# The second layer of a two-layer model run in halves of two blocks, with layer norm and routing of one half beside expert tiles of another

## The chip, the cores and the metric

One core of a Trainium2 chip runs the whole program in one launch. The metric is the device time in microseconds (us) from launch to end; the median of several runs is compared, and smaller is better. Everything is in float32, with each matrix product made of three matmuls on a high part and a low part of its operands (below).

## What is computed

The input is 2,048 tokens of width 128 (4 sequences of 512). Each of two layers adds half a feed-forward, a mixer, and half a feed-forward again to the residual `x`, each on a layer norm of `x`. In layer 0 the feed-forward is a dense one and the mixer a selective scan; in layer 1, which the change is about, they are 64 routed experts with shared ones, and causal attention with 8 heads:

```python
x = x + 0.5 * _L1_ffn_ref(_layernorm(x), ...)   # experts
x = x + _L1_attn_ref(_layernorm(x), ...)        # attention, each sequence of 512 by itself
x = x + 0.5 * _L1_ffn_ref(_layernorm(x), ...)   # the same experts again

rw = _route(x, gate_w, gate_bias)      # per token: best 4 of 8 groups, best 8 experts in them
expert_out = vmap(lambda gw, uw, dw: (silu(x @ gw.T) * (x @ uw.T)) @ dw.T)(Wg, Wu, Wd)
out = einsum('eth,te->th', expert_out, rw) + _mlp(x, Sg, Su, Sd)
```

All experts are computed for all tokens and weighted by `rw`, which is zero for those not chosen. 64 experts of 88 rows are taken as 44 chunks of 128 rows.

## The kernel before

The residual `x` stays in SBUF, 128 features by 2,048 tokens, cut into NB = 4 blocks of T = 512 tokens, one for each sequence. The program is six stages one after the other, with a barrier between them (`end_phase`, `start_phase`: each engine waits for the other four's last work): feed-forward, scan, feed-forward, experts, attention, experts. There is no scheduler: each engine's instructions stand in the order in which the code writes them, and semaphores tie them together.

**Split operands.** `split_hi` (ScalarE) copies a tile into its high part, `split_lo` (GpSimd, in places VectorE) writes full minus high, and `mm3` issues three matmuls (lines 219 to 221).

**The experts' tiles.** A tile is one chunk of 128 expert rows by one block of 512 tokens; an expert stage has 8 tiles of the shared experts and then 44 x 4 = 176 tiles. For tile t TensorE (PE) makes `gate` in PSUM bank 4, once `silu` of tile t-1 has read it, and `up` in bank 5, once `gated` of tile t-1 has read it, each three matmuls; then `down` of tile t-3 (AHEAD = 3), three more. ScalarE (ACT) makes `silu` (line 985); VectorE (DVE) makes `gated` = silu x up (line 1160) and `weighted` = gated x the token's weights in `rwb` (line 1171); ACT splits the high part, GpSimd (POOL) the low part, `e_lo` (line 227). The chunk's weights arrive in `e_raw` by DMA, and ACT and POOL split them into `eh` and `el`. The loop over chunk pairs has 8 tiles: two chunks (two buffers), each against four blocks.

**The start of an expert stage.** Nothing of it is made before the stage. TensorE does the layer norm (a matmul for the mean, small ones for the variance, a matmul to spread the deviation), of all four blocks or, in the first expert stage, of the last one, and the routing logits; then DVE makes the routing of all 16 groups of 128 tokens in 25 steps (lines 1102 to 1151), each of which waits for the one before it, with the 8 shared tiles between. TensorE turns the result, ACT writes it into `rwt`, SyncE (SP) stores it to memory and loads it back, one row spread over the expert's partitions, into `rwb`. The first expert tile waits for that.

**Attention** does the layer norm of all four blocks, then block by block 8 heads; `o_lo` is the low part of one head's output on POOL.

**Tables.** Silu, Sqrt, Sigmoid, Gelu and Exp are in tables of ACT; `load_table` brings one in by a tiny activation.

## Time and profile before

| | |
|---|---|
| time, median of 3 runs | 1790.04 us (1789.91 to 1793.42) |
| the profiled execution, its own time | 1788.16 us |
| its span, first to last instruction | 1786.4 us |
| TensorE matmul busy | 1614.6 us, 90% |
| VectorE busy | 1227.8 us, 69% |
| ScalarE busy | 955.5 us, 53% |
| GpSimd busy | 897.1 us, 50% |
| TensorE's granted clock, mean | 0.947 of 2.4 GHz |
| moved by DMA | 118.7 MB |

A busy share is a mean over stages that are limited by different things, so it is read stage by stage. A matmul of 512 columns shows as 0.39 us but the next one starts 0.23 us after it, so starts, and not durations, tell what one costs on TensorE. What an engine's idle time is worth is told by who waits for it.

### The profile page before, as it was taken

What the parts mean: (1) busy time and instruction counts of PE and PEld (TensorE: products, weight loads), DVE (VectorE), ACT (ScalarE), POOL (GpSimd) and SP (SyncE); (2) the same over time, 40 slices, a digit from 0 to 9 for tenths busy, and PEclk for the clock granted to TensorE, in tenths of its full rate; (3) what the DMA queues carried; (4) which work ended last, traced back from release to release, by engine and by line L of the source; (5) the groups of instructions that cost most, each with busy time, mean ns of one, the idle gap of its engine ahead of it and who ended that gap; (6) DMA issues with size and microseconds to landing.
All of it is one profiled execution on the core that took longest, in us unless ns stands there. A gap on an engine that the chain in (4) does not pass through costs nothing.

```text
span 1786.4 us, 25495 instructions
## 1 busy us (share of the span) xinstructions
PE 1614.6 (90%) x6840; PEld 1208.8 (68%) x6840; DVE 1227.8 (69%) x2015; ACT 955.5 (53%) x1866; POOL 897.1 (50%) x786
## 2 busy tenths in 40 slices
PE   8997577787899975999999998999998699999998
PEld 6775323333377754888888876898875488888887
DVE  5555699999755564666666666787766466666666
ACT  4344645454334342565656555777763256556565
POOL 1001076666410042777777773434323277777776
PEclk9998789999899987999999998999997699999999
DMA  2000000000000003666667640000000367767765
GB/s 102 10 0 1 0 1 1 0 0 0 7 1 1 0 36 84 147 150 152 146 154 150 144 105 1 1 0 0 0 10 1 91 144 152 152 147 152 148 150 120
DMA packets 30035, 118.72 MB, mean 66 GB/s; under 512 B 5323, under 2 KB 17059, under 8 KB 18211
## 3 DMA queue, kind: packets, MB, share of 16 engines
q1 hardware_dynamic: 29987, 118.15, 29.8%
q8 instruction: 22, 0.36, 0.1%
q14 instruction: 26, 0.21, 0.0%
HBM read 116.03 MB, written 2.10 MB: 66 GB/s over the span
## 4 chain that ended last, share of the span: by engine, by line
PE 66%; DVE 3%; issue 2%; POOL 2%; ACT 2%; DMA 1%; POOLq 0%; DVEq 0%; SPq 0%; ACTq 0%
PE ps L219 19%; PE ps L220 18%; PE ps L221 18%; PE ps L1292 2%; PE ps L1277 1%; PE ps L1279 1%; PE ps L1278 1%; PE ps L643 1%; POOL m_hc L853 1%; PE ps L242 1%; DMA rwb<-rw_rows 1%; PE ps L255 1%; POOL e_lo L227 1%; PE ps L249 1%; PE ps L1280 1%
## 5 line engine op out<-in xcount | busy, mean ns | idle before, releaser
L227 POOL TENSOR_TENSOR e_lo<-e_h,e_hi 128x512 fp32r<-128x512 f32 (+1 forms) x368 | 478.5, 1300 | 259.3 <-ACT e_hi L224 252.2
L1160 DVE TENSOR_TENSOR ps<-e_s,ps 128x512 f32<-128x512 f32 x352 | 245.1, 696 | 239.4 <-PE ps L221 179.8
L985 ACT ACTIVATE e_s<-ps 128x512 f32<-128x512 f32 (+1 forms) x368 | 220.5, 599 | 324.6 <-PE ps L221 324.5
L219 PE MATMUL ps<-xn_hi,eh 128*128 128x512 f32 x704 | 280.6, 399 | 22.6 <-DVE ps L1160 22.6
L220 PE MATMUL ps<-xn_lo,eh 128*128 128x512 f32 x704 | 280.8, 399 | 0.0
L221 PE MATMUL ps<-xn_hi,el 128*128 128x512 f32 x704 | 276.4, 393 | 0.0
L1171 DVE TENSOR_TENSOR e_h<-ps,rwb 128x512 f32<-128x512 f32 x352 | 243.3, 691 | 44.7 <-DMA rwb<-rw_rows 21.0
L224 ACT ACTIVATE e_hi<-e_h 128x512 fp32r<-128x512 f32 (+1 forms) x368 | 229.0, 622 | 47.5 <-DVE e_h L1171 25.5
L853 POOL TENSOR_TENSOR m_hc<-m_h,m_c 128x512 f32<-128x512 f32 x128 | 172.8, 1350 | 124.9 <-DVE m_h L809 122.5
L643 PE MATMUL ps<-m_hc,const 128*128 128x512 f32 x256 | 149.6, 667 | 48.8 <-POOL m_hc L853 43.9
L219 PEld LDWEIGHTS ps<-xn_hi,eh 128*128 128x128 f32 x704 | 133.7, 190 | 55.0 <-DVE ps L1160 24.8
L227 POOL TENSOR_TENSOR xn_lo<-ln_c,xn_hi 128x512 fp32r<-128x512 f32 (+1 forms) x24 | 32.9, 1370 | 273.8 <-ACT xn_hi L224 273.8
L221 PEld LDWEIGHTS ps<-xn_hi,el 128*128 128x128 f32 x704 | 134.1, 190 | 31.3
L220 PEld LDWEIGHTS ps<-xn_lo,eh 128*128 128x128 f32 x704 | 133.8, 190 | 31.5
L809 DVE TENSOR_TENSOR_SCAN m_h<-ln_t,ps 128x512 f32<-128x512 f32 x128 | 154.5, 1208 | 0.5 <-ACT ln_t L717 0.5
L219 PE MATMUL ps<-e_hi,eh 128*128 128x512 f32 x352 | 140.0, 398 | 2.4 <-POOL e_lo L227 2.4
L221 PE MATMUL ps<-e_hi,el 128*128 128x512 f32 x352 | 140.6, 399 | 0.0
L220 PE MATMUL ps<-e_lo,eh 128*128 128x512 f32 x352 | 136.8, 389 | 0.0
L219 PE MATMUL ps<-hid_hi,wh 128*128 128x512 f32 x288 | 122.1, 424 | 5.9 <-DVE hid_lo L227 5.0
L643 PEld LDWEIGHTS ps<-m_hc,const 128*128 128x128 f32 x256 | 40.2, 195 | 115.1 <-POOL m_hc L853 114.4
L221 PE MATMUL ps<-hid_hi,wl 128*128 128x512 f32 x288 | 113.1, 393 | 0.0
L220 PE MATMUL ps<-hid_lo,wh 128*128 128x512 f32 x288 | 113.0, 392 | 0.0
(239 smaller groups left out, 3180.5 us busy)
## 6 DMA issues: line engine op xcount, KB each, us to landing
rwb<-rw_rows SPq DMA_DIRECT2D x32, 704.0 KB
rwb<-rw_rows SPq DMA_DIRECT2D x40, 512.0 KB
e_raw<-in_experts SPq DMA_DIRECT2D x88, 192.0 KB, 5.5
rwb<-rw_rows SPq DMA_DIRECT2D x16, 640.0 KB
rwb<-rw_rows SPq DMA_DIRECT2D x24, 384.0 KB
rwb<-rw_rows SPq DMA_DIRECT2D x16, 448.0 KB
rwb<-rw_rows SPq DMA_DIRECT2D x16, 320.0 KB
rwb<-rw_rows SPq DMA_DIRECT2D x40, 128.0 KB
```

Source lines behind the costliest of these rows:

```text
L219: pe.matmul(out, w_hi, x_hi, start=start, stop=False, skip_group_check=True)
L220: pe.matmul(out, w_hi, x_lo, start=False, stop=False, skip_group_check=True)
L221: return pe.matmul(out, w_lo, x_hi, start=False, stop=stop, skip_group_check=True)
L224: return act.activation(hi, full, ACT.Identity)
L227: return eng.tensor_tensor(lo, full, hi.bitcast(F32), ALU.subtract)
L643: pe.matmul(ps[:, 4 + m, :], ident, m_hc[:, q % DEEP, :], start=(n == 0), stop=(n == DS - 1), skip_group_check=True).then_inc(M["y_sum"], 1)
L809: dve.tensor_tensor_scan(m_h[:, q % DEEP, :], m_da[:, q % DEEP, :], ps[:, B_BANKS[q % DEEP], :], 0.0, ALU.mult, ALU.add).then_inc(M["h"], 1)
L853: pool.tensor_tensor(m_hc[:, q % DEEP, :], m_h[:, q % DEEP, :], m_c[:, n % 2, :], ALU.mult).then_inc(M["hc"], 1)
L985: act.activation(e_s[0:rows_, buf, :], ps[0:rows_, 4, :], ACT.Silu).then_inc(S["silu"], 1)
L1160: dve.tensor_tensor(ps[0:rows_, 6 + buf % 2, :], e_s[0:rows_, buf, :], ps[0:rows_, 5, :], ALU.mult).then_inc(S["gated"], 1)
L1171: dve.tensor_tensor(e_h[:, j % 4, :], ps[:, 6 + j % 2, :], rwb[:, j // NB, cut(j % NB)], ALU.mult).then_inc(S["weighted"], 1)
L1292: last = pe.transpose(pt_at(kb)[:, (r - kb) * P:(r - kb + 1) * P], p32[:, r, kb * P:(kb + 1) * P], ident)
```

## The change

Layer 1 is run in halves of two blocks. The stages after the second feed-forward are now E1A (first experts, blocks 0 and 1), attention 0, E1B (first experts, blocks 2 and 3), attention 1, E2A (second experts, blocks 0 and 1), E2B (second experts, blocks 2 and 3). Layer norm and routing are made beside the tiles of the stage before:

- The second feed-forward also makes the routing of blocks 0 and 1 (on DVE after the splits of its blocks 2 and 3) and the logits of blocks 0 to 2; E1A makes the layer norm of block 3 and the routing of blocks 2 and 3; E1B both for blocks 0 and 1 of the second experts; E2A both for blocks 2 and 3.
- `beside(t)` on each engine puts a piece after tile t: means, variances and spreads in the free banks 2 and 3, logits after t = 14 and 15, routing on DVE in five pieces (`route_pairs`, `route_groups`, `route_mask`, `route_top`, `route_weights`) after t = 17, 18, 20, 21, 23 for one block and 26, 27, 29, 31, 32 for the other. A block's routing is 24 steps on 4 groups of tokens; before it was 25 steps on 16. The first SIDE = 4 rounds of 8 tiles are written out for it, and the others are a loop.
- A chunk now has two tiles and not four, and is loaded, and split, four times and not twice. There are four buffers. The low part of the down weights is now made by DVE (`down_low`), and that of gate and up stays with POOL. `rwb` holds 1,024 tokens a chunk.
- The attention's weights are split in 8 parts beside tiles of E1A, the low parts by DVE (`attention_low`).
- The layer norm of the first block of an attention half stands at the end of the experts before it, and that of its second block beside the attention's start. Attention and both feed-forwards are written out block by block instead of in loops.

```diff
-        TILES = 2 * NB + CH * NB
-        ROUTE_STEPS = 25
+        TILES = 4 + 2 * CH
+        ROUTE_STEPS = 24
...
+        SHARED, PER, AHEAD, SLOTS = 4, 8, 3, 4
+        ROUNDS = CH // SLOTS
+        SIDE = 4
...
             def beside(t):
+                if t == 7:
+                    if first in L[1]:
+                        one_deviation(act, L[0], first, 2)
+                    one_deviation(act, L[0], second, 3)
+                    load_table(act, ACT.Silu)
...
+                if t == 16:
+                    if first in L[1]:
+                        route_scores(act, R, first, 2)
+                    route_scores(act, R, second, 3)
+                    load_table(act, ACT.Silu)
...
+            def down_low(i, c):
+                dve.wait_ge(*S("wd_hi", SLOTS * i + c + 1))
+                split_lo(dve, el[:, c, 0, :], e_raw[:, c, 0, :], eh[:, c, 0, :]).then_inc(S["wd_lo"], 1)
...
+                if t in (17, 26):
+                    route_pairs(dve, R, first if t == 17 else second)
+                if t in (18, 27):
+                    route_groups(dve, R, first if t == 18 else second)
+                if t in (20, 29):
+                    route_mask(dve, R, first if t == 20 else second)
...
+            def round_(i):
+                for j in range(PER):
+                    tile(i, j)
+                    if j in (0, 2, 4):
+                        down_low(i, 1 + j // 2)
+                    if j == 6:
+                        down_low(i + 1, 0)
+                    if isinstance(i, int):
+                        beside(in_round(i, j))
...
-            moe_pe(pe, E1, LN[3], True)
+            moe_pe(pe, E1A, 0, R1, (LN[3], (3,)), (2, 3), LN4A)
             end_phase(pe)
             start_phase(pe, 4)
-            att_pe(pe, LN[4])
+            att_pe(pe, LN4A, 0)
             end_phase(pe)
             start_phase(pe, 5)
-            moe_pe(pe, E2, LN[5], False)
+            moe_pe(pe, E1B, 1, R2, (LN5A, (0, 1)), (0, 1), LN4B)
+            end_phase(pe)
+            start_phase(pe, 6)
+            att_pe(pe, LN4B, 1)
+            end_phase(pe)
+            start_phase(pe, 7)
+            moe_pe(pe, E2A, 0, R2, (LN5B, (2, 3)), (2, 3), None)
+            end_phase(pe)
+            start_phase(pe, 8)
+            moe_pe(pe, E2B, 1, R2, None, None, None)
             end_phase(pe)
```

VectorE before, in the first expert stage: steps of the routing of all blocks (`r_t`, `r_u`, `r_small`), with products of shared tiles (`e_h<-e_s,ps`) between, ahead of any expert tile.

```order
L1110 TENSOR_TENSOR r_u<-r_t 128x256 [waits moe_route]
L1076 TENSOR_TENSOR e_h<-e_s,ps 88x512 [waits moe_silu,moe_up]
L1111 TENSOR_TENSOR r_t<-r_t 128x256 [waits moe_route]
L1112 TENSOR_TENSOR r_t<-r_u 128x256 [waits moe_route]
L1113 TENSOR_TENSOR r_u<-r_u,r_t 128x256 [waits moe_route]
L1076 TENSOR_TENSOR e_h<-e_s,ps 88x512 [waits moe_silu,moe_up]
```

VectorE now, in E1B after tile 17: the first routing piece of block 0 stands between the products of expert tiles 17 and 18 (`ps<-e_s,ps` is `gated`, `e_h<-ps,rwb` is `weighted`), and a split of weights (`el<-e_raw,eh`, `down_low`) and the second piece behind tile 18.

```order
L463 TENSOR_TENSOR r_c<-r_s,rows 128x256 [waits route_scores]
L467 TENSOR_TENSOR r_t<-r_c 128x128 [waits route_route]
L468 TENSOR_TENSOR r_u<-r_c 128x128 [waits route_route]
L471 TENSOR_TENSOR r_u<-r_t 128x64 [waits route_route]
L472 TENSOR_TENSOR r_t<-r_t 128x64 [waits route_route]
L473 TENSOR_TENSOR r_t<-r_u 128x64 [waits route_route]
L1277 TENSOR_TENSOR ps<-e_s,ps 128x512 [waits moe_silu,moe_weighted,moe_up,route_route]
L1282 TENSOR_TENSOR e_h<-ps,rwb 128x512 [waits moe_rw_in3,moe_h_lo,moe_gated]
L234 TENSOR_TENSOR el<-e_raw,eh 128x128 [waits moe_wd_hi]
L477 TENSOR_TENSOR r_u<-r_u,r_t 128x64
```

What moved: steps a quarter as wide, but as many for each block, now stand in VectorE's queue ahead of the next tile's `gated`.

ScalarE now, in E1B after tile 16: two table loads (to Sigmoid and back to Silu) stand around the scores, between `e_hi` of tile 16 and `silu` (`e_s<-ps`) of tile 18.

```order
L231 ACTIVATE e_hi<-e_h 128x512 [waits moe_down,moe_weighted]
L1123 ACTIVATE eh<-e_raw 128x128 [waits moe_down]
L426 ACT_TABLE_LOAD
L426 ACTIVATE r_s<-ps 128x256 [waits route_logits] x2
L240 ACT_TABLE_LOAD
L240 ACTIVATE unused<-cols 128x1
L1129 ACTIVATE e_s<-ps 128x512 [waits moe_gated,moe_gate]
```

What moved: the scores of a stage (`r_s`) were made before its first tile, and their table was loaded where no `silu` waited.

TensorE now, at the end of E1A: the mean of block 0 for the attention ahead of the last `down`, its variance and spread behind it, and then the barrier.

```order
L361 MATMUL ps<-x,mean_w 128x512 [waits route_rwt,moe_x_new]
L226 MATMUL ps<-e_hi,eh 128x512 [waits moe_h_lo]
L227 MATMUL ps<-e_lo,eh 128x512
L228 MATMUL ps<-e_hi,el 128x512
L367 MATMUL ps<-mean_w,ln_t 128x1 [waits ln_squared]
L367 MATMUL ps<-mean_w,ln_t 128x1 x3
L372 MATMUL ps<-ln_t,mean_w 128x512 [waits ln_diag]
L226 MATMUL ps<-xn_hi,ah 128x512 [waits ln_xn_lo,a_lo,phase_end]
```

What moved: one block's layer norm is now made behind the last tiles of the stage, where before four were made at the start of the attention.

## Rows read from the trace of the kernel before

**Rows 1.** Stages: us, busy PE, PEld, DVE, ACT, POOL; clock, DMA share, GB/s

```profile
631.30:703.00 71.70, 44.57 (x164) 30.81 (x164) 37.55 (x86) 22.20 (x38) 21.51 (x14) 0.75 0.21 56
703.00:1066.70 363.70, 363.70 (x1563) 295.05 (x1563) 241.85 (x349) 215.88 (x435) 273.99 (x261) 0.99 0.67 144
1070.80:1334.60 263.80, 248.09 (x1516) 217.08 (x1516) 197.08 (x479) 187.57 (x472) 100.28 (x82) 0.97 0.00 1
1334.60:1415.50 80.90, 57.62 (x199) 37.94 (x199) 40.35 (x98) 23.73 (x43) 18.61 (x14) 0.69 0.15 36
1415.50:1779.50 364.00, 363.97 (x1563) 295.48 (x1563) 241.77 (x349) 215.96 (x435) 273.85 (x261) 0.99 0.67 144
```

**Rows 2.** One expert tile in the timeline: start, duration, engine, line, names, idle before

```profile
899.60 1.29 POOL L227 TENSOR_TENSOR e_lo<-e_h,e_hi 128x512 fp32r<-128x512 f32 x1 [0.79 <-ACT e_hi L224]
899.83 0.69 DVE L1171 TENSOR_TENSOR e_h<-ps,rwb 128x512 f32<-128x512 f32 x1
901.27 0.70 DVE L1160 TENSOR_TENSOR ps<-e_s,ps 128x512 f32<-128x512 f32 x1 [0.76 <-PE ps L221]
902.37 0.40 PE L219 MATMUL ps<-xn_hi,eh 128*128 128x512 f32 x1
```

**Rows 3.** Groups by form, 800 to 1000 us: busy, mean ns of one

```profile
L227 POOL TENSOR_TENSOR e_lo<-e_h,e_hi 128x512 fp32r<-128x512 f32 x97 | 125.5, 1294 | 49.3 <-ACT e_hi L224 47.3
L227 POOL TENSOR_TENSOR el<-e_raw,eh 128x256 fp32r<-128x256 f32 x24 | 17.8, 743 | 0.0
```

**Rows 4.** Routing steps of the first expert stage on VectorE, timeline

```profile
652.45 0.42 DVE L1112 TENSOR_TENSOR r_t<-r_u 128x256 f32<-128x256 f32 x1
654.80 0.28 DVE L1117 TENSOR_TENSOR r_small<-r_t 128x128 f32<-128x128 f32 x1
670.65 2.12 DVE L1139 MAX8 r_small<-r_c 128x8 f32<-128x64 f32 x16
```

**Rows 5.** VectorE and GpSimd at once in the same stage, timeline

```profile
650.85 1.28 POOL L227 TENSOR_TENSOR e_lo<-e_h,e_hi 88x512 fp32r<-88x512 f32 x1 [3.33 <-ACT e_hi L224]
651.37 1.05 DVE L1111 TENSOR_TENSOR r_t<-r_t 128x256 f32<-128x256 f32 x1
...
663.23 5.09 POOL L227 TENSOR_TENSOR al<-a_raw,ah 128x2304 fp32r<-128x2304 f32 x1
663.90 4.49 DVE L1134 TENSOR_SCALAR r_small<-r_small 128x128 f32<-128x128 f32 x1
668.28 1.26 POOL L227 TENSOR_TENSOR e_lo<-e_h,e_hi 88x512 fp32r<-88x512 f32 x1
```

**Rows 6.** A table load on ScalarE, timeline

```profile
645.77 1.28 ACT L985 ACT_TABLE_LOAD   x1
```

**Rows 7.** TensorE after a wait for VectorE, timeline of the first expert stage

```profile
664.04 0.73 PE L219 MATMUL ps<-xn_hi,sh 128*88 128x512 f32 x1 [2.15 <-DVE e_h L1076]
```

**Rows 8.** Logits on TensorE, timeline

```profile
633.32 0.28 PE L879 MATMUL ps<-sl,xn_hi 128*128 128x64 f32 x1
633.43 0.28 PE L880 MATMUL ps<-sh,xn_lo 128*128 128x64 f32 x1
```

**Rows 9.** Layer norm of the attention's first block: first mean and last low part

```profile
1070.79 1.98 PE L242 MATMUL ps<-x,mean_w 128*128 128x512 f32 x4 [0.83 <-DVEq L208]
1079.48 1.27 POOL L227 TENSOR_TENSOR xn_lo<-ln_c,xn_hi 128x512 fp32r<-128x512 f32 x1 [10.54 <-ACT xn_hi L224]
```

**Rows 10.** Attention: its first key, and the first head's output in blocks 0 and 3

```profile
1088.84 0.69 DVE L1437 SCALAR_TENSOR_TENSOR kv<-ps,k_add 128x512 f32<-128x512 f32 x1
1108.88 1.29 POOL L227 TENSOR_TENSOR o_lo<-o,o_hi 128x512 fp32r<-128x512 f32 x1 [3.94 <-ACT o_hi L224]
1285.18 1.30 POOL L227 TENSOR_TENSOR o_lo<-o,o_hi 128x512 fp32r<-128x512 f32 x1 [3.16 <-ACT o_hi L224]
```

**Rows 11.** End of the second feed-forward on VectorE: last split, and the new residual

```profile
628.69 0.69 DVE L227 TENSOR_TENSOR hid_lo<-f_h,hid_hi 128x512 fp32r<-128x512 f32 x1
630.43 0.75 DVE L548 SCALAR_TENSOR_TENSOR x<-ps,w_half,x 128x512 f32<-128x512 f32 x1 [1.06 <-PE ps L221]
```

More of the change, by code:

```diff
@@ new lines, in route_scores, with route_turn @@
+        def route_scores(act, R, b, bank):
+            act.wait_ge(*R("logits", b + 1))
+            act.activation(r_s[:, b, :, :].rearrange("p t e -> p (t e)"), ps[:, bank, 0:4 * E], ACT.Sigmoid).then_inc(R["scores"], 1)
+        def route_turn(pe, R, b, bank):
+            pe.wait_ge(*R("route", ROUTE_STEPS * (b + 1)))
+            for t in range(4):
+                last = pe.transpose(ps[0:E, bank, t * P:(t + 1) * P], r_t[:, t * E:(t + 1) * E], ident)
+            last.then_inc(R["rw_t"], 1)
@@ new lines, in route_rows @@
+        def route_rows(act, R, b, bank):
+            act.wait_ge(*R("rw_t", b + 1))
+            if R is R2:
+                act.wait_ge(*R1(f"rw_out{b // 2}", 16))
+            act.activation(rwt[:, cut(b)], ps[0:E, bank, :], ACT.Identity).then_inc(R["rwt"], 1)
+        NGT = 4 * NG
+        r_k = [r_small[:, k, :] for k in range(4)]
+        r_c8 = r_c[:, :, :].rearrange("p t (g k) -> p (t g) k", k=8)
+        r_t3 = r_t[:, :].rearrange("p (t e) -> p t e", e=E)
+        r_u3 = r_u[:, :].rearrange("p (t e) -> p t e", e=E)
@@ L898, in gate_up, with in_round, moe_pe @@
+        SHARED, PER, AHEAD, SLOTS = 4, 8, 3, 4
+        ROUNDS = CH // SLOTS
+        SIDE = 4
+        ORDERED = tuple((j // 2, j % 2) for j in range(PER))
+        CLOSING = ((0, 0), (0, 1), (1, 0), (1, 1), (2, 0), (3, 0), (2, 1), (3, 1))
+        FREE_BANKS = (2, 3)
+        def in_round(i, j):
+            return PER * i + SHARED + j
+        def moe_pe(pe, S, half, R, L, ahead, N):
+            first, second = ahead or (None, None)
             def gate_up(t, gh, gl, uh, ul, b, rows_):
+                blk = cut(2 * half + b)
@@ new lines, in round_ @@
+                    if j == 1:
+                        gate_up_high(i, 3)
+                    if j in (3, 5, 7) and not last:
+                        gate_up_high(i + 1, (j - 3) // 2)
+                    if j in (4, 6) and not last:
+                        down_high(i + 1, (j - 4) // 2)
+                    if isinstance(i, int) and not last:
+                        beside(t)
+            begun = SIDE if ahead else 0
+            for i in range(begun):
+                round_(i, False)
+            with act.Fori(begun, ROUNDS - 1) as i:
+                round_(i, False)
@@ new lines, in moe_pool_tiles, with moe_dve @@
+            begun = SIDE if ahead else 0
+            for i in range(begun):
+                round_(i, False)
+            with pool.Fori(begun, ROUNDS - 1) as i:
+                round_(i, False)
+            round_(ROUNDS - 1, True)
+            if N:
+                one_low(pool, N, 2 * half)
+        def moe_dve(dve, S, half, R, L, ahead, N):
+            first, second = ahead or (None, None)
+            def down_low(i, c):
+                dve.wait_ge(*S("wd_hi", SLOTS * i + c + 1))
+                split_lo(dve, el[:, c, 0, :], e_raw[:, c, 0, :], eh[:, c, 0, :]).then_inc(S["wd_lo"], 1)
@@ L1147, in moe_dve, with tile @@
-            total = small[3][:, 0:NTT]
-            step(dve.tensor_reduce(total, u3, AX, ALU.add))
-            step(dve.tensor_scalar(total, total, 1e-20, None, ALU.add))
-            step(dve.reciprocal(total, total))
-            step(dve.scalar_tensor_tensor(t3, u3, 2.5, total.unsqueeze(2).broadcast_to([P, NTT, E]), ALU.mult, ALU.mult))
-            assert steps[0] == ROUTE_STEPS
-            def gate(t, buf, rows_):
+            def tile(i, j, tiles=ORDERED):
+                c, b = tiles[j]
+                t, buf, bank = in_round(i, j), j % 4, 6 + j % 2
@@ new lines, in x_new @@
+            def x_new(b):
+                blk = cut(2 * half + b)
+                dve.wait_ge(*S("down", in_round(ROUNDS - 1, CLOSING.index((3, b))) + 1))
+                dve.scalar_tensor_tensor(x[:, blk], ps[:, b, :], 0.5, x[:, blk], ALU.mult, ALU.add).then_inc(S["x_new"], 1)
+            begun = SIDE if ahead else 0
+            for i in range(begun):
+                round_(i)
+            with dve.Fori(begun, ROUNDS - 1) as i:
+                round_(i)
+            for j in range(PER):
+                tile(ROUNDS - 1, j, CLOSING)
+                if j in (0, 2, 4):
+                    down_low(ROUNDS - 1, 1 + j // 2)
```

952 lines of the change are left out of this document (530 added, 422 removed).

## Prediction

> **What bounds the kernel now.** I read the busy time by stage first, because the shares of the whole span hide the stages. In the two long stretches of expert tiles TensorE is busy all the time at a clock of 0.99: 363.7 and 364.0 us, 1,563 matmuls each [rows 1]. That is 0.233 us a matmul and, with nine to a tile, 2.09 us a tile; the other engines are busy two thirds of it or three quarters. The starts of the two expert stages are different: 71.7 and 80.9 us in which TensorE does 164 and 199 records at a clock of 0.75 and 0.69 [rows 1]. There the routing on VectorE and the trip of its result through memory end last. The attention, 263.8 us, is 94% TensorE [rows 1]. From 631.3 us on the span has 1,155.1 us: 263.8 of attention and 891.3 of experts. The experts' 368 tiles need 368 x 2.09 = 770 us, so that 121 us are what the change can save there at most.
>
> The second view is the timeline of one tile, because the new pieces stand between tiles. `weighted` ends at 899.83 + 0.69 = 900.52, `gated` of the next tile starts at 901.27 after 0.76 us idle and ends at 901.97, and the `up` that overwrites its bank starts at 902.37 [rows 2]. So VectorE may be late once by 0.76 + 0.40, less some 0.06 for the signal: 1.1 us. What goes beyond it TensorE waits, one for one, since `up` stands in its queue ahead of all that follows. The lead of three tiles covers `down` only, and bank 5 has no second buffer.
>
> **The change, term by term, against the 1,786.4 us span (own time 1,788.2).**
>
> *Removed.* The 121 us of starts, ends and barriers of the expert stages, all of it; what takes its place follows.
>
> *TensorE's own pieces.* Layer norm of a block is three steps near 1.0 us (two means are four records and 1.98 us [rows 9]); logits 12 matmuls 0.11 apart, 1.3 [rows 8]; four transposes I take at 0.15, 0.6. E1A has one layer norm, one set of logits and two turns, 5.5; E1B and E2A have two of each, 9.8. Together 25 us, none hidden, for TensorE bounds.
>
> *Table loads.* At t = 7 and t = 16 ScalarE waits for TensorE's last variance or logits, then has a small activation (0.3), a load (1.28 [rows 6]), the tiny one (0.2) and the waiting `silu` (0.6), and `gate` waits for that: 2.5 us with the signals. Twice in three stages: 15 us.
>
> *Layer norm on VectorE.* Centring and normalising wait for a matmul that TensorE has just done, and `gated` stands behind them: 0.69 + 0.70 + 0.2 of signals less the `gate` that runs meanwhile (0.69), 0.9 each; ten of these and the diagonals: 12 us.
>
> *Routing on VectorE.* 256 columns take 0.42 and 128 take 0.28 [rows 4], with 0.04 between dependent steps, so 64 take about 0.25 and 32 about 0.22; sixteen maxima take 2.12 [rows 4], four 0.53, and the replacements as much. The five pieces of a block come to 1.85, 1.3, 2.3, 1.3 and 1.8 us, 8.6 in all. From it go the 1.1 us of slack and what the six tiles in the stretch give back. A tile leaves VectorE 2.09 - 1.39 = 0.7, and `down_low` takes about 0.3 in every second one; I take 0.4 a tile, 2.4. That leaves 5.1 us. To it comes GpSimd: a VectorE step that began at 651.37 beside a 1.28 us subtraction on GpSimd took 1.05 where its like took 0.42, and ended 0.3 after it; another took 4.49 beside one of 5.09 [rows 4, 5]. GpSimd has 1.29 + 0.74/2 = 1.66 us to do in a tile [rows 3], against 1.59 now, and the low part of the same tile always falls into a piece that is longer than 1 us. In four of five pieces I put 1.0 us for it; the bounds are nothing and 1.7 (its weight split too). So 9.1 us a block, and six blocks are routed beside tiles: 55 us. The Trainium skill, in "SBUF — State Buffer", section "Who interferes with whom", states that a DVE instruction with two SBUF inputs and a GpSimd one that reads SBUF exclude each other for the whole instruction. By that rule, with which these rows agree, the term stands; without any lock the total below would be 24 us less. It is a rule against this change, which puts such instructions on VectorE beside a busier GpSimd.
>
> *Attention's weights.* Eight splits of 288 columns with two inputs in SBUF, about 0.47 us and a wait each, half of them in tiles that have room: 6 us.
>
> *Clock.* After 2.15 us of waiting for VectorE a matmul took 0.73 [rows 7], where it is 0.40 at the full clock [rows 2]: the lower of the two levels. Some pieces stop TensorE that long. 2 us a stage, 6 us; bounds 0 and 18.
>
> *Filling, draining.* Four stages instead of two: 2.6 us each to fill (three tiles with nothing behind them, twice at the lower clock after an attention), 2.8 each at the end (now 4.1 us from 1066.7 to 1070.8, of which 2.1 are matmuls, and the barrier): 21.5 us, and 3 us of output at the end.
>
> *Layer norm behind the tiles.* From first mean to last low part it now takes 1079.48 + 1.27 - 1070.79 = 10.0 us [rows 9]. At the end of E1A and E1B one block's stands there, with a load of Sqrt in it; a little lies beside the last `down`: 10 us each, 20 us. The weights' first loads and the row weights come early enough: they are asked for in the stage before.
>
> Experts now: 770 + 25 + 15 + 12 + 55 + 6 + 6 + 21.5 + 3 + 20 = 933.5, against 891.3: +42.
>
> *Attention.* From its first key to the first head's output 20.0 us pass; from there blocks 0 to 2 take (1285.18 - 1108.88)/3 = 58.8 each, and the last 49.4 to the end at 1334.6 [rows 10]. A half has 1.5 to the key, 20.0, and a layer norm beside the start, whose variance and spread stand in TensorE's queue ahead of the second query and the first heads and whose two table loads stand ahead of the first exponentials: 8 us. Twice (29.5 + 58.8 + 49.4) = 275.4: +12.
>
> *Second feed-forward.* Three logits, 4 us. At the ends of blocks 2 and 3 the last 3.1 us of routing stand after the last split (629.38), so that the residual comes near 632.5 and not 630.43 [rows 11]; turn and copy follow, and the next block's `up` or the barrier waits: 3.3 each. +10.6. The first 5.5 us of routing lie in a gap of as much between the splits of two layers.
>
> *Steady tiles.* `down_low` (0.28 by its like [rows 4]) waits until GpSimd's low part ends at 900.89 and fits ahead of `gated` at 901.27 [rows 2]; GpSimd at 1.66 of 2.09 us keeps up; cover gone, see the second rival. Cost nothing. The chunk weights, 192 KB of 1.2 MB before, are moved twice as often: the DMA share of 0.67 [rows 1] goes to 0.78.
>
> Sum: +42 + 12 + 10.6 = +65, 1,853 us for the profiled execution. The median of runs lay 1.9 us above it, well inside the uncertainty of the terms: I say **1,852 us**. With the bounds of the lock (-24, +17), of the clock (-6, +12) and a third of the rest the case has 1,805 to 1,890.
>
> **Rivals.**
>
> *The lead hides the pieces (faster).* If `up` is hardly held, because VectorE runs ahead of TensorE by more than I see, tables, layer norm, routing, weights and clock (94 us) vanish: 1,759 us. For it: three tiles of lead, and 1,228 us busy of 1,786 on VectorE. Against it: at 664.04 TensorE stood 2.15 us for just this product with routing ahead of it [rows 7], and the idle before `gated` is only 0.76. It decides where no more than 29 of the 94 us are left. 17%.
>
> *GpSimd's split goes first (slower still).* If GpSimd's next instruction, the 0.74 us weight split [rows 3], takes its turn before the waiting `down_low`, `gated` starts 0.7 late, 0.35 of that beyond `up`'s slack, once in each of 176 chunks: +62, 1,915 us. Against it: a VectorE step that had waited since 663.90 ended at 668.39, while GpSimd's next instruction, 1.26 long, began at 668.28 [rows 5], so the waiting one went first. The skill's same section says that issue order decides. 12%.
>
> *DMA.* If a row of half the length costs its packets the same time, the row weights fill the queues, some 5 us a chunk against 4.2: 1.5 us in 176 chunks, over 2,050 us. Bytes in Rows 1 speak for time by size. 3%.
>
> *Gains and losses nearly cancel*, with no waits for GpSimd and half of the table and layer norm stops: 1,780 to 1,805. 10%; within 0.2% 4% of all.
>
> **How the numbers follow.** 58% for my forecast, 17, 12, 3 and 10 for the others. A change under 0.2% (3.6 us) can't be told here. Slower 58 + 12 + 3 + 5 = 78%, within it 4%, faster 18%. The range 1,780 to 1,905 reaches some way towards the lead case and into the lock case, and leaves out about 2 in 10.
>
> **What would show it.** The stages of tiles: E2B near 184 + 8 us at 2.09 a tile; E1A, E1B and E2A 30 to 45 us longer, with TensorE waiting for DVE `gated` in the waits list (some 60 us) and for ACT `e_s` (15 us). VectorE steps of 0.2 us that take 1 to 1.5 beside `e_lo`. Wrong would be I if tiles 17 to 35 ran at 2.09 (lead), if the loop rounds ran above 2.09 (lock), or if VectorE waited for `rwb` in the loops (DMA).

## The result, and the profile after

The changed kernel takes 1845.97 us (median of 4 runs, 1843.78 to 1849.99) where the kernel before, on the same chip, takes 1791.73 (4 runs, 1789.91 to 1793.9). The ratio is 1.0305 with a 95% interval of 1.0280 to 1.0329: 54 us slower. The profiled execution was the longest of the four, 1849.99 us, with a span of 1848.2.

Some of its 61.8 us over the span of before belong to no change, and have to come off first. Two windows near the start, and TensorE's row between them (start, duration, idle time and its releaser):

```profile
10.00:15.00 5.00, 5.00 (x20) 3.97 (x19) 2.24 (x4) 2.52 (x5) 2.18 (x1) 0.50 0.88 357
15.00:20.00 5.00, 5.00 (x13) 2.93 (x13) 2.25 (x4) 1.47 (x3) 1.46 (x2) 0.50 0.04 15
```

```profile
8.62 1.39 PE L249 MATMUL ps<-x,mean_w 128*128 128x512 f32 x2 [1.88 <-DMA x<-in_x]
```

The load of `x` landed late, TensorE stood 1.88 us for it (0.53 in the profiled run of before, where the clock here was 1.00), and the next 10 us ran at the lower clock, 0.50 of 2.4 GHz. The first residual came 6.3 us late (64.33 us here, 58.07 before): the first matmul began 1.8 us later (8.62 and 6.85), and the rest was run at the lower clock. The change leaves the work up to there as it is. That the wait lowered the clock is not shown: in the trace of experiment 7 TensorE stood 2.50 us for the same load and the clock stayed at 1.00 from 5 to 15 us, in that of experiment 8 it stood 1.01 and the clock was 0.50 from 10 to 15. The traces of experiments 1 to 8 have this residual at 59.1 to 61.1 us, and in all ten the last residual before the experts ends between 643.4 and 646.9 us, here at 650.2. Without the 6.3 us the trace holds 55.5 us, which agrees with the 54 of the medians.

The stages, to be read beside [rows 1] (us, busy PE, PEld, DVE, ACT, POOL with records; clock, DMA share, GB/s). In order: E1A, attention 0, E1B, attention 1, E2A, E2B:

```profile
650.80:892.70 241.90, 214.57 (x873) 164.14 (x873) 176.96 (x311) 141.49 (x297) 154.14 (x138) 0.95 0.59 150
892.70:1029.10 136.40, 125.71 (x747) 108.96 (x747) 97.14 (x237) 93.32 (x235) 47.71 (x37) 0.95 0.01 2
1029.10:1274.20 245.10, 220.11 (x897) 168.87 (x897) 173.60 (x307) 138.92 (x292) 155.16 (x139) 0.94 0.51 131
1274.20:1411.30 137.10, 127.33 (x747) 110.73 (x747) 97.72 (x237) 93.27 (x235) 47.25 (x37) 0.94 0.00 1
1411.30:1649.20 237.90, 216.30 (x884) 167.09 (x884) 172.12 (x302) 136.13 (x289) 153.92 (x138) 0.95 0.51 129
1649.20:1848.20 199.00, 194.27 (x828) 154.07 (x828) 145.84 (x226) 125.07 (x272) 151.98 (x136) 0.99 0.62 157
```

The four expert stages have 92 tiles each and the two attention stages 16 heads each, so they can be compared with each other. E2B has nothing beside its tiles and takes 199.0 us at a clock of 0.99; E1A, E1B and E2A do side work and take 42.9, 46.1 and 38.9 us more, at 0.94 to 0.95. The two starts of [rows 1], 71.7 and 80.9 us, are gone, and these took their place.

A steady tile is unchanged. Two tiles in a loop round of E2A, on VectorE, beside [rows 2]:

```profile
1589.48 0.69 DVE L1277 TENSOR_TENSOR ps<-e_s,ps 128x512 f32<-128x512 f32 x1 [0.16 <-PE ps L228]
1591.57 0.70 DVE L1277 TENSOR_TENSOR ps<-e_s,ps 128x512 f32<-128x512 f32 x1 [0.67 <-PE ps L228]
1592.91 0.58 DVE L234 TENSOR_TENSOR el<-e_raw,eh 128x128 fp32r<-128x128 f32 x1
1593.66 0.70 DVE L1277 TENSOR_TENSOR ps<-e_s,ps 128x512 f32<-128x512 f32 x1 [0.17 <-PE ps L228]
```

`gated` starts every 2.09 us, TensorE's own pace, and still waits for TensorE each time; `down_low`, 0.58 long where it alone would be 0.28, eats most of VectorE's gap and no more. So everything is lost beside the tiles that are written out. The list of waits from 640 us to the end (us in total, times, longest) names two holders:

```profile
PE ps L226 <- DVE ps L1277: 38.8, 32, 2.9
PE ps L226 <- ACT e_s L1129: 21.9, 10, 3.4
PE ps L1482 <- DVE p L1655: 7.7, 10, 2.1
```

The starts of `gated` tell where: over 2.09 us a tile, tiles 4 to 88 are late by 33.5 us in E1A, 38.0 in E1B and 38.1 in E2A, and by 0.2 in E2B. In E2A 12.4 of it lie in tiles 5 to 13 (layer norm and its tables), 5.9 at tile 18 (two sets of logits, a table exchange), and the rest from there to tile 37. One of ten routing pieces of E2A, VectorE and GpSimd together:

```profile
1472.84 0.78 POOL L234 TENSOR_TENSOR el<-e_raw,eh 128x256 fp32r<-128x256 f32 x1
1472.95 0.75 DVE L477 TENSOR_TENSOR r_u<-r_u,r_t 128x64 f32<-128x64 f32 x1
1473.74 0.19 DVE L481 TENSOR_TENSOR r_small<-r_t 128x32 f32<-128x32 f32 x1
1473.93 1.27 POOL L234 TENSOR_TENSOR e_lo<-e_h,e_hi 128x512 fp32r<-128x512 f32 x1 [0.31 <-ACT e_hi L231]
1473.96 1.29 DVE L482 TENSOR_TENSOR r_small<-r_t 128x32 f32<-128x32 f32 x1
1475.29 0.19 DVE L483 TENSOR_TENSOR r_small<-r_u 128x32 f32<-128x32 f32 x1
```

Two steps with the same form, 32 elements, take 0.19 and 1.29 us. The long one began 0.03 us after GpSimd's 1.27 us subtraction and ended 0.05 after it. The step at 1472.95 did the same with a weight split. Against the shortest step of the same form, twelve of the 48 steps are lengthened in this way in each of E2A and E1B, by 7.9 and 8.0 us together, and eleven in E1A, by 7.9: 23.8 us in all.

The second feed-forward, its four residuals beside [rows 11], and TensorE's largest wait in it:

```profile
537.87 0.75 DVE L668 SCALAR_TENSOR_TENSOR x<-ps,w_half,x 128x512 f32<-128x512 f32 x1 [2.07 <-PE ps L228]
574.61 0.75 DVE L668 SCALAR_TENSOR_TENSOR x<-ps,w_half,x 128x512 f32<-128x512 f32 x1 [3.97 <-PE ps L228]
611.45 0.75 DVE L668 SCALAR_TENSOR_TENSOR x<-ps,w_half,x 128x512 f32<-128x512 f32 x1 [0.78 <-PE ps L228]
649.47 0.75 DVE L668 SCALAR_TENSOR_TENSOR x<-ps,w_half,x 128x512 f32<-128x512 f32 x1
```

```profile
PE ps L226 <- ACT r_s L426: 3.3, 2, 1.7
```

From residual to residual the blocks take 36.7, 36.8 and 38.0 us where they took 33.8, 33.7 and 32.3: 11.8 us more. The last residual has no idle time before it: VectorE came to it late, from the routing.

### The profile page after: what moved, and what is told of

The parts are those of the page before. It is cut to its first block, busy times and chain, and to the rows that moved or that the text cites. A ratio compares the mean times of both kernels' runs of the same rounds, so it can differ in the third digit from the quotient of the medians.

```text
span 1848.2 us, 25319 instructions
## 1 busy us (share of the span) xinstructions
PE 1644.0 (89%) x6840; PEld 1214.3 (66%) x6840; DVE 1343.7 (73%) x2332; ACT 1018.9 (55%) x2065; POOL 917.7 (50%) x779
## 4 chain that ended last, share of the span: by engine, by line
PE 60%; DVE 8%; ACT 3%; issue 3%; POOL 2%; POOLq 1%; DMA 0%; ACTq 0%; DVEq 0%; SPq 0%
PE ps L226 17%; PE ps L227 16%; PE ps L228 16%; DVE ps L1277 2%; PE ps L1482 2%; PE ps L1467 1%; DVE e_h L1282 1%; PE ps L1468 1%; PE ps L1469 1%; PE ps L766 1%; POOL m_hc L976 1%; POOL e_lo L234 1%; ACT L240 1%; PE ps L367 1%; POOLq L215 1%
## 5 line engine op out<-in xcount | busy, mean ns | idle before, releaser
L226 PE MATMUL ps<-xn_hi,eh 128*128 128x512 f32 x704 | 293.7, 417 | 57.3 <-DVE ps L1277 38.8
L227 PE MATMUL ps<-xn_lo,eh 128*128 128x512 f32 x704 | 285.3, 405 | 0.0
L228 PE MATMUL ps<-xn_hi,el 128*128 128x512 f32 x704 | 283.8, 403 | 0.0
L234 POOL TENSOR_TENSOR el<-e_raw,eh 128x256 fp32r<-128x256 f32 x176 | 137.7, 782 | 29.9 <-ACT eh L1118 29.9
L234 POOL TENSOR_TENSOR xn_lo<-ln_c,xn_hi 128x512 fp32r<-128x512 f32 x24 | 34.1, 1421 | 229.6 <-ACT xn_hi L231 229.6
L227 PE MATMUL ps<-e_lo,eh 128*128 128x512 f32 x352 | 141.5, 402 | 0.0
```

Of the source, the lines that this page charges most:

```text
L226: pe.matmul(out, w_hi, x_hi, start=start, stop=False, skip_group_check=True)
L227: pe.matmul(out, w_hi, x_lo, start=False, stop=False, skip_group_check=True)
L228: return pe.matmul(out, w_lo, x_hi, start=False, stop=stop, skip_group_check=True)
L234: return eng.tensor_tensor(lo, full, hi.bitcast(F32), ALU.subtract)
```

## The experiments

Differences are between medians, against 1845.97 us for the changed kernel unless another is named; the runs of one kernel lie within 1.2 to 7.6 us of each other, those of the kernel before within up to 15. The ratio is to the kernel before on the same chip (1791.3 us in experiments 1 to 4, 1790.84 in 5 to 8, 1790.33 in 9 and 10). What tiles lose is what the starts of their `gated` fall behind 2.09 us a tile, counted from the first of the two tiles named. The theory is that of the prediction: TensorE is held because VectorE has more to do beside the tiles than they leave it, a part of it standing still beside GpSimd, and because `up` has one bank. The rivals are given with each.

### 1. A second bank for `up`

```diff
-                pe.wait_ge(*S("gated", t))
-                mm3(pe, ps[0:rows_, 5, :], uh, ul, ...)
+                pe.wait_ge(*S("gated", t - 1))
+                mm3(pe, ps[0:rows_, 5 + 2 * (par % 2), :], uh, ul, ...)
```

> `up` goes alternately to banks 5 and 7 and `gated` always to bank 6, so that VectorE may be late by one more tile, 3.2 us and not 1.1, before TensorE is held. Nothing is left out. My theory: TensorE is held because VectorE has more to do beside tiles 17 to 34 than the tiles leave it, so that a bank more is a debt paid once: about 4 us for each stage's routing and 2 for its layer norm, 1846 - 18 = 1828 us (1820 to 1836). Rival: it is only the missing bank, each piece being late by itself and made good before the next; then nearly all of the holds for VectorE (some 65 us) go and the time is near 1785. Nothing changes (1846) if TensorE is held by something else, such as ScalarE or GpSimd.

1826.07 us, ratio 1.0191 (1.0149 to 1.0233): 20 us less, near the 18 of the theory and far from the rival's 61. The waits from 640 us on:

```profile
PE ps L226 <- ACT e_s L1129: 31.6, 28, 3.7
PE ps L226 <- DVE ps L1277: 21.6, 18, 2.0
```

The wait for VectorE fell from 38.8 to 21.6 us, and that for ScalarE rose from 21.9 to 31.6. That the sum came near is partly luck, for its parts are the wrong way round. The theory had 12 us in the three stages' routing and 6 in their layer norm; the starts of `gated` gained 4.2 in tiles 17 to 40, where the routing stands, and 10.1 in tiles 4 to 17, with the layer norm and its tables. A buffer forgives lateness once; VectorE's debt over tiles 17 to 34 is longer than a tile, and `silu`, with one bank for `gate`, is next.

### 2. The routing left out beside the tiles

```diff
-                if t in (17, 26):
-                    route_pairs(dve, R, first if t == 17 else second)
-                ...
+                if t in (23, 32):
+                    dve.tensor_tensor(r_t3, r_s[:, b, :, :], bias, ALU.add).then_inc(R["route"], ROUTE_STEPS)
```

> Leaves out 23 of the 24 steps of each block's routing on VectorE beside the tiles of E1A, E1B and E2A (one addition stands for them), so that the row weights are not the reference's; the routing of blocks 0 and 1 in the second feed-forward stays, and so do logits, scores, turns and row loads. My theory (routing on VectorE holds TensorE 9.1 us a block): 1846 - 55 = 1791 us (1786 to 1798). If the lead hid the pieces it would stay at 1846; if only the lock with GpSimd cost, 24 us of it would go, 1822.

1794.45 us, ratio 1.0021 (1.0005 to 1.0037): 51.5 us less, where the prediction's term was 55. It is as much as the whole loss but 3 us: without the routing on VectorE the other new costs (tables, layer norm, logits, fill and drain) would about use up what the removed starts gave. In the trace 45.7 us of it lie in tiles 17 to 40.

### 3. No table exchange beside the tiles

```diff
-                    one_deviation(act, L[0], second, 3)
-                    load_table(act, ACT.Silu)
+                    one_deviation(act, L[0], second, 3, ACT.Identity)
-                    route_scores(act, R, second, 3)
-                    load_table(act, ACT.Silu)
+                    route_scores(act, R, second, 3, ACT.Silu)
```

> The deviation and the scores beside tiles use functions of the table that silu needs (Identity for Sqrt, Silu for Sigmoid) and the four loads of each stage are gone; deviations and scores are therefore not the reference's. My theory: 2.5 us at t = 7 and t = 16 in three stages, 1846 - 15 = 1831 us (1827 to 1837). Rival: behind the table stands VectorE, late by its own piece, so that only the first of the two matters: half of it, 1838. If silu's lead hid the loads: 1846.

1828.2 us, ratio 1.0205 (1.0163 to 1.0246): 17.8 us less, a mean of 3.0 for each of six exchanges, near the 15 of the theory. The two of a stage are not alike. Tile 18, behind the exchange at t = 16, loses 1.5 us less in each stage, so that one costs as well, but half of the mean; tiles 4 to 17, with the exchange at t = 7, lose 2.8 us less in E1A and 3.9 in E1B and E2A. Of the 3.9, in E2A, 2.1 are two tiles behind the exchange (9 to 11), which take 4.3 us at a clock of 1.00 where in the changed kernel they take 6.4 at 0.55. TensorE's wait for `e_s` in E2A fell from 6.2 to 3.1 us, that for `gated` stayed (13.3 and 13.6).

### 4. One step behind each tile

```diff
-                if t in (17, 26):
-                    route_pairs(dve, R, first if t == 17 else second)
-                ...
+                for begin, b in ((17, first), (37, second)):
+                    if begin <= t < begin + len(GROUPS):
+                        for k in GROUPS[t - begin]:
+                            route_steps(dve, R, b)(k)
```

> The 24 routing steps of a block stand in 18 groups of one or two steps, one group behind each tile from 17 to 34 and, for the other block, from 37 to 54; 8 rounds are written out and not 4, the attention's low parts stand behind tiles 58 to 65, and the rows are stored later. Nothing is left out. My theory: a step of 0.42 us waits for GpSimd's low part until 0.37 us after `weighted` and then ends about when `gated` could begin, so that it fits into the 1.1 us of slack: of the 55 us of routing some 10 stay, 1846 - 45 = 1801 us (1795 to 1810). Rival: a tile now asks 1.39 + 0.14 + 0.42 us and a lock of up to 1 us from VectorE, more than 2.09, so that the debt is the same but spread: 1835 or more.

1811.81 us, ratio 1.0117 (1.0076 to 1.0158): 34 us less, of the 51.5 that routing costs; I had expected 45 and at most 1810. The rival is not right either (1835). In this stretch tiles take alternately 1.8 and 2.7 us, 4.53 for two where TensorE's pace is 4.18. A tile of E2A with both a weight split and a step shows why:

```profile
1463.60 1.30 POOL L234 TENSOR_TENSOR e_lo<-e_h,e_hi 128x512 fp32r<-128x512 f32 x1 [1.05 <-ACT e_hi L231]
1464.59 0.46 DVE L234 TENSOR_TENSOR el<-e_raw,eh 128x128 fp32r<-128x128 f32 x1
1464.85 0.79 POOL L234 TENSOR_TENSOR el<-e_raw,eh 128x256 fp32r<-128x256 f32 x1
1464.97 0.96 DVE L562 SCALAR_TENSOR_TENSOR r_t<-r_t,r_u 128x256 f32<-128x256 f32 x1
1465.96 0.69 DVE L1341 TENSOR_TENSOR ps<-e_s,ps 128x512 f32<-128x512 f32 x1
```

VectorE's split waited for `e_lo` and went first; then GpSimd's weight split, itself stretched from 0.74 to 0.79, took its turn; the step behind it waited and took 0.96 instead of 0.42. In E2A 15 steps are lengthened by 0.2 us or more, by 8.0 together, most of them right behind a `down_low`. Experiment 7 follows from this.

### 5. The second input from PSUM

```diff
+            def tt(out, a, b, op):
+                return dve.tensor_tensor(out, a, from_psum(b), op)
+            def stt(out, a, c, b, op0, op1):
+                return dve.scalar_tensor_tensor(out, a, c, from_psum(b), op0, op1)
-                t, buf, bank = in_round(i, j), j % 4, 6 + j % 2
+                t, buf, bank = in_round(i, j), j % 4, 6
```

> In the routing pieces beside the tiles of E1A, E1B and E2A each step with two inputs in SBUF reads its second input from PSUM (bank 7, whose contents are not the reference's numbers; `gated` always writes bank 6), so that the row weights of the experts are wrong, while the number, sizes and places of the steps stay. My theory (steps with two inputs in SBUF stand still beside GpSimd's subtractions; in E2A the lengthened routing steps lose 7.4 us together): no step is lengthened any more, three stages of 6 us less and 0.03 us a step more for PSUM: 1846 - 15 = 1831 us (1826 to 1836), with no step of 0.2 us that takes more than 0.35. Rival: the long steps come from something else that GpSimd's work goes with (semaphores, SBUF write port, the tables), so that they stay: 1846. By the Trainium skill, SBUF — State Buffer, section Who interferes with whom, a VectorE instruction with at most one input in SBUF does not contend with GpSimd; by it the steps are short.

1818.43 us, ratio 1.0152 (1.0131 to 1.0174): 27.5 us less, more than the 15 expected and outside its range, and near the prediction's 24 (4 x 1.0 us in six blocks). The same work at the same places, on VectorE and GpSimd (two answers of the timeline, the second GpSimd's):

```profile
1453.31 0.41 DVE L553 TENSOR_TENSOR r_t<-r_small,ps 128x256 f32<-128x256 f32 x1
1453.76 0.42 DVE L556 SCALAR_TENSOR_TENSOR r_u<-r_t,ps 128x256 f32<-128x256 f32 x1
1454.21 0.42 DVE L556 SCALAR_TENSOR_TENSOR r_t<-r_t,ps 128x256 f32<-128x256 f32 x1
1454.66 0.42 DVE L574 TENSOR_REDUCE r_small<-r_t 128x32 f32<-128x256 f32 x1
```

```profile
1453.20 0.79 POOL L234 TENSOR_TENSOR el<-e_raw,eh 128x256 fp32r<-128x256 f32 x1
1454.15 1.28 POOL L234 TENSOR_TENSOR e_lo<-e_h,e_hi 128x512 fp32r<-128x512 f32 x1 [0.16 <-ACT e_hi L231]
```

Four steps run beside two subtractions of GpSimd, and none is longer than 0.42; in E1A, E1B and E2A no step is lengthened at all, and the 0.03 us a step that the expectation adds for PSUM is not to be seen. So the lock with GpSimd is shown as the cause of the long steps, and for these steps, with two inputs, the second one's place in SBUF as its condition. It is not the only condition there is: the step of [rows 5] that took 4.49 us beside GpSimd is a TENSOR_SCALAR, with one input, and its like in the second expert stage took 0.22. The Trainium skill, "SBUF — State Buffer", section "Who interferes with whom", says that a VectorE instruction with at most one SBUF input, outside the two-port modes, does not contend with GpSimd; the trace agrees for the steps here, with 0.41 to 0.42 us in the rows above.

Why 27.5 us went where the lengthened steps add up to 23.8, the starts of `gated` tell, which gained 27.5 too: 22.9 of it lie in tiles 18 to 40, where the routing stands, and 4.6 in tiles 9 to 13, where none does. There the same two tiles of E2A, 9 to 11, ran at the lower clock for the most part in the changed kernel and not here (the first row is the changed kernel's):

```profile
1440.65:1447.04 6.39, 6.33 (x16) 5.04 (x17) 4.26 (x7) 2.88 (x7) 3.25 (x3) 0.55 0.49 114
1418.01:1422.27 4.26, 4.21 (x17) 3.15 (x18) 4.16 (x7) 3.16 (x8) 3.27 (x3) 1.00 0.36 97
```

TensorE's stop before them is the same in both traces (tile 9 loses 4.7 us), so what decided the clock is open; the price of the lock, with the clock that its stops cost, is about 23 us.

### 6. `down_low` on GpSimd

```diff
             def low(t, buf, rows_):
...
+                    if j in (0, 2, 4):
+                        down_low(i, 1 + j // 2)
+                    if j == 6 and not last:
+                        down_low(i + 1, 0)
```

> The low part of the down weights is made by GpSimd and not by VectorE, at the same places; nothing is left out. My theory: VectorE has nine splits less in tiles 17 to 34 of each stage, 0.28 to 0.6 us each, and TensorE is held that much less, about 3.5 us a stage; in the loop rounds GpSimd has 1.29 + 0.37 + 0.2 = 1.87 us of work in 2.09 and still keeps up: 1846 - 10 = 1836 us. Rival: GpSimd at 90% makes `e_lo` late, TensorE waits for it before `down`, and tiles take 2.2 us and not 2.09: 264 tiles in loops, 1846 + 25 = 1871.

1843.9 us, ratio 1.0295 (1.0270 to 1.0320): 2 us less, which is no difference. Neither number came: loop tiles stay at 2.09 us, so GpSimd keeps up, and yet TensorE gained nothing from nine splits less on VectorE. A part of the time came back as lock: in E2A 19 steps are lengthened, by 9.5 us, where it was 12 by 7.9. Two of them:

```profile
1473.15 0.96 POOL L234 TENSOR_TENSOR el<-e_raw,eh 128x256 fp32r<-128x256 f32 x1
1473.55 0.85 DVE L494 SCALAR_TENSOR_TENSOR r_u<-r_t,const 128x256 f32<-128x256 f32 x1
1474.34 1.28 POOL L234 TENSOR_TENSOR e_lo<-e_h,e_hi 128x512 fp32r<-128x512 f32 x1 [0.23 <-ACT e_hi L231]
1474.43 1.47 DVE L495 SCALAR_TENSOR_TENSOR r_t<-r_t,r_u 128x256 f32<-128x256 f32 x1
```

Two steps of 0.42 us took 0.85 and 1.47. Where two engines exclude each other, moving work between them moved little here; what became of the rest of the time was not tested.

### 7. Routing behind odd tiles, two banks for `up`

```diff
-        GROUPS = 18 groups, one behind each tile from 17 and from 37
+        GROUPS = [[1, 2], [3, 4, 5], [6, 7, 8], [9, 10, 11], [12, 13], [14, 15],
+                  [16, 17], [18], [19], [20, 21], [22, 23], [24]]
+                    if t % 2 and 0 <= (t - begin) // 2 < len(GROUPS):
```

The lines are against experiment 4 (the first is shortened), and the banks of `up` are those of experiment 1. Nine rounds are written out, the attention's low parts stand behind tiles 68 to 75, and the turns of the two blocks' results behind tiles 40 and 66.

> Routing steps only behind odd tiles, 17 to 39 and 43 to 65, in 12 groups of one to three steps (even tiles have `down_low`, behind which GpSimd's weight split took its turn before the step), and `up` alternately in banks 5 and 7; nothing is left out. My theory: a pair of tiles asks 2 x 1.42 + 0.46 + 0.8 = 4.1 us of VectorE and fits into 4.18, so that routing costs nothing more, as when it was left out (1794), and the second bank takes some 2 to 3 us of the layer norm's holds in each stage: 1787 us (1782 to 1795). Rival: each step still meets a subtraction of GpSimd and costs the lock, as with one step a tile: 1805.

1783.54 us, ratio 0.9960 (0.9947 to 0.9973): 62 us less than the changed kernel, and faster than before the change. TensorE's waits for VectorE's `gated` no longer appear among the six largest, and tiles 18 to 40 lose 3.3 us in the three stages, where it was 60.0. The lock did not go: the rival is right that steps still meet GpSimd's subtraction (14 of 48 in E2A, by 4.5 us), but it costs nothing, for it falls into time that VectorE has. With nothing left out the kernel is 11 us below the one without routing and with one bank, more than the 7 expected of the bank.

### 8. Two banks for `gate` as well

```diff
+                mm3(pe, ps[0:rows_, 4 + 2 * (par % 2), :], gh, gl, ...)
-                dve.tensor_tensor(ps[:, bank, :], e_s[:, buf, :], ps[:, 5, :], ALU.mult)
+                dve.tensor_tensor(ps[:, bank, :], e_s[:, buf, :], ps[:, bank, :], ALU.mult)
```

The lines are against experiment 7, some of them shortened.

> As the kernel with routing behind odd tiles, but `gate` alternately in banks 4 and 6 and `up` in banks 5 and 7, `gated` written over `up`; nothing is left out. My theory: silu may now be late by a tile too, so that most of the 2.5 us of each table exchange is hidden as well: 1787 - 10 = 1777 us (1770 to 1785), faster than before the change. Rival: the exchange holds TensorE because the work behind it (`gated` of the same tiles) is late as well, and VectorE keeps its bank 0.7 us longer: no gain over two banks, 1787 to 1792.

1767.05 us, ratio 0.9863 (0.9842 to 0.9884): 16.5 us less again, more than expected (1770 us at least). That this is about the price of the tables (17.8) does not mean that they are hidden: against experiment 7, tiles 4 to 17 lose 10.5 us less and the tiles before them 3.3, while tile 18, behind the exchange at t = 16, loses as much as in the changed kernel (5.9 us in E1B and E2A). Its E2A, and a stretch of it with all of its routing beside tiles:

```profile
1354.20:1565.90 211.70, 205.88 (x884) 161.30 (x884) 172.79 (x302) 136.54 (x288) 153.41 (x138) 0.99 0.58 146
1398.00:1500.00 102.00, 98.88 (x436) 78.94 (x435) 91.41 (x178) 66.95 (x142) 75.45 (x70) 1.00 0.65 161
```

E2A fell from 237.9 to 211.7 us and its clock rose from 0.95 to 0.99. VectorE is busy 91 of 102 us in that stretch and TensorE 99: the same work, but spread so that it fits. What doesn't go is the lock: in the three stages 49 steps are lengthened by 0.2 us or more, by 25.0 us together, more than the 23.8 of the changed kernel, and yet tiles 18 to 40 lose only 5.1 us. One of them, again with 32 elements:

```profile
1419.72 1.29 POOL L234 TENSOR_TENSOR e_lo<-e_h,e_hi 128x512 fp32r<-128x512 f32 x1 [0.23 <-ACT e_hi L231]
1419.80 1.27 DVE L558 TENSOR_TENSOR r_small<-r_small 128x32 f32<-128x32 f32 x1
```

So a lengthened step costs TensorE only where VectorE has no time left for it.

### 9. Four banks with the pieces at their old places

The edit is the banks of experiment 8 (two for `up`, two for `gate`) on the changed kernel.

> `gate` in banks 4 and 6, `up` in 5 and 7, `gated` over `up`, with the routing pieces in their places behind tiles 17 to 32 as in the changed kernel; nothing is left out. My theory: the second gate bank hides most of the table exchanges (15 us) beyond what the second bank of `up` did (20 us), but the debt of the routing stays: 1826 - 14 = 1812 us (1806 to 1820), so that of the 79 us between the changed kernel and the one with routing behind odd tiles about 45 are the places and 34 the banks. Rival: with two banks of each the places no longer matter: 1775 or less.

1810.47 us, ratio 1.0117 (1.0089 to 1.0145), as expected. Of the 79 us between the changed kernel and experiment 8, the banks alone bring 35.5 and the places (of the routing, and with it of the turns and the attention's low parts), once the banks are there, 43.4. The banks alone don't do it. In the starts of `gated` they gained 19.9 us in tiles 4 to 17 and only 4.2 in tiles 17 to 40; in E2A TensorE still waits for VectorE:

```profile
PE ps L226 <- DVE e_h L1283: 14.6, 10, 2.6
```

### 10. The logits of the second feed-forward in bank 2

```diff
-                            route_logits(pe, R, N, i - 1, 0)
+                            route_logits(pe, R, N, i - 1, 2)
-                            if R and i:
+                        if k == 2 and R and i:
                                 pe.wait_ge(*R("scores", i))
```

> As the kernel with four banks and routing behind odd tiles, and in the second feed-forward the logits go to bank 2 and not to bank 0, so that the first two gates of the next block no longer wait for the scores; nothing is left out. My theory: of the 11.9 us by which the second feed-forward is longer, 1.7 in each of two blocks are this wait: 1767 - 3.5 = 1763.5 us (1762 to 1766). Rival: the gates are then held at bank 2 instead, or the next block's silu is what waits for ScalarE, which makes the scores and two tables first: 1767.

1767.04 us, ratio 0.9859 (0.9834 to 0.9884), where experiment 8 has 1767.05: no change, and outside the range expected. The wait for the scores is gone, and the residuals, beside those of experiment 8's trace, show where the gain went:

```profile
531.76 0.75 DVE L731 SCALAR_TENSOR_TENSOR x<-ps,w_half,x 128x512 f32<-128x512 f32 x1 [2.07 <-PE ps L228]
566.63 0.75 DVE L731 SCALAR_TENSOR_TENSOR x<-ps,w_half,x 128x512 f32<-128x512 f32 x1 [2.06 <-PE ps L228]
602.76 0.75 DVE L731 SCALAR_TENSOR_TENSOR x<-ps,w_half,x 128x512 f32<-128x512 f32 x1
641.94 0.75 DVE L731 SCALAR_TENSOR_TENSOR x<-ps,w_half,x 128x512 f32<-128x512 f32 x1
```

The first interval shrank by 1.9 us and the second by 0.7, and the third grew by 1.2, from 38.0 to 39.2: the last two residuals have VectorE's routing directly before them, and TensorE now waits for `r_t` (3.5 us, was 2.2). Some 1.5 us were left in this trace, too little for the medians. Whether more would come by routing these two blocks elsewhere was not tried.

## Why the prediction was right

It said 1852 us and the time is 1846; of the +62 us over the median shown then, 54 came. (Its sum gives 1853 for the profiled execution, and with the 1.9 us to the median 1855.) By its own steps:

- **The mechanism.** "What goes beyond it TensorE waits, one for one": the two rivals without it fell. *The lead hides the pieces* (1759 us) would be seen in tiles 17 to 35 at 2.09 us; tile 21, behind a routing piece, took 5.6, and tile 18, behind logits, tables and a piece, 7.95. *Gains and losses nearly cancel* needed no waits for GpSimd; twelve in one stage are there.
- **Steady tiles cost nothing.** Right: 2.09 us a tile in all loop rounds. In *GpSimd's split goes first*, what I feared for the steady tiles doesn't happen: the waiting `down_low` goes first, and takes at most 0.6 us. It does happen to the instruction behind it, which in steady tiles isn't a subtraction (experiment 4). The DMA rival fell with the same rows; its price was wrong as well, since 5 us a chunk against 4.2 is 0.8 us in 176 chunks, 1,994 us, and not 1.5. The DMA share is 0.62 in E2B, 0.65 at 164 GB/s in its tiles alone (1655 to 1835 us), and not 0.78, so that figure was too high, though it entered no sum.
- **Routing on VectorE, 55 us.** 51.5 by experiment 2. Of it the lock was put at 24; the lengthened steps add up to 23.8, and experiment 5 gives 27.5, of which 22.9 lie in the tiles with routing. That it came so near is partly luck: I had one wait of 1.0 us in four of five pieces, eight a stage, and there are eleven or twelve of 0.2 to 1.1. The rows behind it say less than I took from them: the step of 4.49 us in [rows 5] has one input, so it does not bear out a rule on two. And the term holds only for these places; in experiment 8 the same lengthening costs next to nothing.
- **Table loads, 15 us.** 17.8 by experiment 3: 3.0 and not 2.5 an exchange in the mean, but 1.5 for the one at t = 16 and the rest for the one at t = 7, with part of it in the lower clock after that.
- **TensorE's pieces, tables, layer norm, routing, attention's weights and clock together.** 119 us (25 + 15 + 12 + 55 + 6 + 6) in the sum, 109.6 in the starts of `gated` (33.5 + 38.0 + 38.1): this is where the sum was too high. The attention's weights were over-sized, 6 us: tiles 20 to 35 lose 15.9 us in E1A, which splits them, and 15.2 in E2A, which doesn't. They seem to have had room in tiles without a piece; no run leaves them out.
- **Filling, draining, output and the closing layer norm.** 44.5 us (21.5 + 3 + 20). The experts took 924.4 us from the last residual of the feed-forward, at 650.3, to the end without the attention's 273.5; less 770 for the tiles and 109.6 that leaves 44.8.
- **Experts as a whole.** +42 predicted; 924.4 against 891.3 is +33.
- **Attention.** +12 predicted (275.4), +9.7 measured (136.4 + 137.1 = 273.5 from the first key of each half to the next stage).
- **Second feed-forward.** +10.6 predicted, +11.8 measured, but the total hides a wrong split: I had 1.3 for each set of logits and 3.3 at the ends of blocks 2 and 3. The end of block 2 costs about nothing (the second interval grew by 3.2), and the first two sets of logits cost, with 1.3 for the matmuls as predicted, 1.65 each for the scores, which were in my sum nowhere. The third interval grew by 5.8; with 1.3 for its logits that leaves 4.5 for the end of block 3.
- **The waits list.** I expected some 60 us for `gated` and 15 for `e_s`; it has 38.8 and 21.9. The stages E1A, E1B and E2A were to be 30 to 45 us longer than E2B and are 42.9, 46.1 and 38.9. A wait is not the whole price of a hold: in E2A up to 1510 us the clock is 0.88, and after a stop matmuls follow each other 0.43 us apart and not 0.23, which the list doesn't count.

So +33, +9.7 and +11.8 make 55 of the change, where the sum had +65; the other 7 us of the profiled span were its late start and 1 us in the scan.

## What to carry to other kernels

Work that is put "beside" a saturated engine is only hidden if each interval has room for it: count what the helper engine has free per tile (here 0.7 us, less in every second tile), and cut the pieces to that before adding buffers; buffers alone brought 35 us of 79, and in the tiles with routing hardly any of it, since they repay a lateness once and not a debt. Before placing a small two-input VectorE step, look at what GpSimd does at that moment, because the step can take what is left of GpSimd's instruction and not its own 0.2 us; where VectorE has that time to spare, it costs nothing (experiment 8). And judge a side piece by leaving it out on the chip, and then look where in the trace the time went: one run told here that the routing costs 51.5 us, and the starts of `gated` told that experiments 1 and 8 came near their sums with other parts than those expected.

## What the runs showed of the hardware

- A VectorE step of 32 elements with both inputs in SBUF took 0.19 us alone and 1.29 beside a GpSimd subtraction of 1.27; with one input in PSUM, and for a reduction with one input, there was no lengthening (0.41 to 0.42 us for 256 columns beside 1.28 us on GpSimd). A TENSOR_SCALAR of 128 elements with one input in SBUF was held all the same: 4.49 us beside a subtraction of 5.09, and 0.22 alone (kernel before, [rows 5]).
- The two engines take turns: when a `down_low` waited for `e_lo`, it went ahead of GpSimd's next instruction, and GpSimd's next came before VectorE's next (0.46 us, then 0.79, then a step at 0.96, experiment 4).
- The same stop of TensorE was followed by the lower clock in one trace and not in another: behind tile 9 of E2A two tiles took 6.39 us at 0.55 and 4.26 at 1.00 (experiment 5), and at the start a wait of 2.50 us was followed by 1.00 and one of 1.01 by 0.50. Traces of one kernel, and times of its runs, differ by as much as small changes are worth.
